# A decoder layer on one core: silu moved ahead of the quantised row on ScalarE, the output norm's scalars first on GpSimd, and one query row tile normed in every step

## The reference, cut to what matters

```
x = x + attn(layernorm(x))     # gated linear scan along the rows (stage 1)
x = x + xattn(layernorm(x))    # 16 heads over 64 context rows and one null key; output projected and normed
x = x + ffn(layernorm(x))      # gate = silu(quant(z) @ ternary(w_gate).T); up likewise;
                               # out = quant(gate * up) @ ternary(w_down).T
quant(v): scale = 127 / max|v| of the row; round(v * scale) / scale
```

## Time and profile before

| | |
|---|---|
| median of 3 runs | 540.6 us (540.0 to 541.85) |
| the profiled execution, its own time | 540.44 us |
| its span | 538.7 us |
| PE busy | 481.4 us (89% of the span) |
| DVE busy | 423.9 us (79%) |
| ACT busy | 324.0 us (60%) |
| POOL busy | 304.4 us (57%) |

### The profile page before, as it was taken

One profiled execution on the slowest core, in us unless ns is written; L12 is line 12 of the kernel. 1 busy time (PEld: TensorE's weight loads), 2 busy tenths in 40 slices (PEclk: granted clock), 3 DMA queues, 4 the chain that ended last, 5 costly groups with the idle time before them and its releaser, 6 DMA issues.

```text
span 538.7 us, 9271 instructions
## 1 busy us (share of the span) xinstructions
PE 481.4 (89%) x2926; PEld 389.4 (72%) x2954; DVE 423.9 (79%) x936; ACT 324.0 (60%) x450; POOL 304.4 (57%) x482
## 2 busy tenths in 40 slices
PE   1889999989988989999999999999999999988662
PEld 0666787767767878788887887888878778866321
DVE  4899998968337676988888888888888888875673
ACT  4422233245333353797788888877878888685451
POOL 2211223710001668778778787887787878787631
PEclk9999999999999999999999999999999999998895
DMA  8995000240000000012321222121213211212242
GB/s 263 321 337 213 1 0 1 40 78 1 2 0 1 1 2 5 12 24 50 42 49 35 44 48 49 35 50 41 49 35 46 48 46 36 54 40 63 51 97 68
DMA packets 68173, 32.06 MB, mean 60 GB/s; under 512 B 50720, under 2 KB 66336, under 8 KB 68128
## 3 DMA queue, kind: packets, MB, share of 16 engines
q1 hardware_dynamic: 68128, 31.50, 23.3%
HBM read 15.24 MB, written 4.19 MB: 36 GB/s over the span
## 4 chain that ended last, share of the span: by engine, by line
POOL 31%; issue 23%; PE 21%; DVE 17%; DMA 4%; ACT 2%; POOLq 1%; DVEq 1%; SPq 0%; ACTq 0%
PE psum L1140 9%; POOL region_d L540 5%; POOL region_d L518 3%; POOL xs L520 3%; POOL region_d L516 3%; PE psum L1156 3%; POOL sc L563 3%; POOL sc L550 3%; DVE region_a L877 3%; PE psum L1382 2%; POOL region_d L574 2%; PE psum L1387 2%; POOL region_d L531 2%; POOL region_c L579 2%; DMA region_d<-region_d 2%
## 5 line engine op out<-in xcount | busy, mean ns | idle before, releaser
L528 POOL TENSOR_TENSOR region_d<-region_d,rden 128x1024 f32<-128x1024 f32 x32 | 60.9, 1902 | 100.7 <-DVE rden L1008 100.7
L1140 PE MATMUL psum<-Mhi,xT2hi 128*128 128x260 f32 x256 | 75.0, 293 | 0.2
L1140 PE MATMUL psum<-Mlo,xT2hi 128*128 128x260 f32 x256 | 72.4, 283 | 0.0
L1140 PE MATMUL psum<-Mhi,xT2lo 128*128 128x260 f32 x256 | 72.3, 282 | 0.0
L1382 PE MATMUL psum<-VW,region_d 128*128 128x256 f32 x256 | 62.6, 389 | 4.6 <-DVE pTn L1057 4.6
L1387 PE MATMUL psum<-VW,region_d 128*128 128x256 f32 x256 | 60.7, 380 | 0.0
L1021 DVE SCALAR_TENSOR_TENSOR region_c<-psum,zw,region_c 128x1024 f32<-128x1024 f32 x29 | 37.2, 1283 | 28.7 <-ACT region_c L698 28.7
L1382 PEld LDWEIGHTS psum<-VW,region_d 128*128 128x128 f32 x256 | 49.0, 193 | 14.9 <-DVE pTn L1057 6.0
L1387 PEld LDWEIGHTS psum<-VW,region_d 128*128 128x128 f32 x256 | 49.0, 191 | 6.8
L686 ACT ACTIVATE region_d<-psum,sc 128x256 f32<-128x256 f32 x32 | 18.0, 564 | 55.7 <-POOL sc L567 54.8
L991 DVE TENSOR_REDUCE mx<-psum 128x8 f32<-128x520 f32 x64 | 44.2, 691 | 6.4 <-PE psum L1140 5.2
(11 more groups left out here) (143 smaller groups left out, 1242.2 us busy)
## 6 DMA issues: line engine op xcount, KB each, us to landing
out_dram<-xs SPq DMA_DIRECT2D x32, 128.0 KB, 1.9
xs<-in_x_dram SPq DMA_DIRECT2D x1, 2560.0 KB, 13.9
VW<-in_L_xattn_Wkv_dram SPq DMA_DIRECT2D x1, 2048.0 KB, 11.9
region_b<-in_L_xattn_Wkv_dram SPq DMA_DIRECT2D x1, 2048.0 KB, 17.6
xs<-in_x_dram SPq DMA_DIRECT2D x3, 512.0 KB, 7.0
region_w<-in_L_ffn_w_gate_dram SPq DMA_DIRECT2D x2, 512.0 KB, 10.3
region_w<-in_L_ffn_w_up_dram SPq DMA_DIRECT2D x2, 512.0 KB, 7.9
region_w<-in_L_ffn_w_down_dram SPq DMA_DIRECT2D x8, 128.0 KB, 4.5
```

The lines of the kernel that those rows point to most:

```text
L528: pool.tensor_tensor(p2[:, v, 0:H * MK].rearrange("p (h j) -> p h j", j=MK), e[:, :, 0:MK], rden[:, v, :].unsqueeze(2).broadcast_to([P, H, ...
L1140: mm = pe.matmul(dst, lhsT, rhs, start=i == 0, stop=i == len(terms) - 1)
```

## The change: what it does

1. silu and the hidden row of a tile now share one buffer, and there are two of these, taken in turn (`hid3`: the two places that were `sg` and `h`). DVE multiplies in place. silu waits for `hq_done` of the tile two before in place of `h_ready` of the one before; DVE's wait for `hq_done` ahead of the hidden row is gone, with the last tiles' detour through `e`.
2. ACT issues silu ahead of the quantised row in all steps, as it did from step 32.
3. POOL issues the output norm's three small operations (L561 to L567) ahead of the feed-forward norm's (L548 to L554).
4. ACT norms one query tile (n+5) in every step from -1 to 26, where it normed two (n+4, n+5) in each even one. The transposes stay in even steps.

```diff
-        sg3 = c["sg"]
+        hid3 = [c["sg"], c["h"]]
...
-        h3 = [c["h"], s["e"][:, 0:FI]]
...
 POOL, stages2_3:
+                if exists(n, T):
+                    ... (L558 to L568 as they were, moved up)
                 if exists(n - 2, T):
                     ... (L543 to L555)
-                if exists(n, T):
-                    ... (L558 to L568)
...
 ACT, silu_gate:
-                if positive(n - 5):
-                    act.wait_ge(h_ready, n - 5)
-                act.activation(sg3, banks(0, 2).rearrange("p b n -> p (b n)"), ACT.Silu,
+                if positive(n - 6):
+                    act.wait_ge(hq_done, n - 6)
+                act.activation(hid3[v], banks(0, 2).rearrange("p b n -> p (b n)"), ACT.Silu,
                                scale=zw[:, (n - 5) % 4, 0:1]).then_inc(silu_ready, 1)
...
 ACT, stages2_3:
-                if late(n) and exists(n - 5, T):
+                if exists(n - 5, T):
                     silu_gate(n, v)
                 if exists(n - 6, T):
...
-                    act.activation(nq3, hidden(n - 6), ACT.Copy, scale=qr[:, u, 0:1]).then_inc(hq_done, 1)
-                if not late(n) and exists(n - 5, T):
-                    silu_gate(n, v)
+                    act.wait_ge(h_ready, n - 5)
+                    act.activation(nq3, hid3[u], ACT.Copy, scale=qr[:, u, 0:1]).then_inc(hq_done, 1)
                 if not late(n) and exists(n - 3, T):
                     norm3(n, v)
-                if even:
-                    act.wait_ge(xT2_psum, half(n) + 1)
-                    norm2(n + 4, 2 * (u4 // 2))
-                    norm2(n + 5, 2 * (u4 // 2) + 1)
+                if exists(n, T - 5) or n == -1:
+                    act.wait_ge(xT2_psum, (n + 1) // 2 + 1)
+                    norm2(n + 5, (n + 5) % 4)
                 if even:
                     xT2_pair(half(n) + 2, u4 // 2)
...
 DVE, hidden_layer:
                 dve.wait_ge(silu_ready, n - 4)
-                if late(n):
-                    dve.wait_ge(hq_done, n - 6)
-                    dve.wait_ge(p_ready, 2 * T)
-                elif positive(n - 5):
-                    dve.wait_ge(hq_done, n - 5)
-                dve.scalar_tensor_tensor(out=hidden(n - 5), ..., in1=sg3, ...)
+                dve.scalar_tensor_tensor(out=hid3[v], ..., in1=hid3[v], ...)
```

More of the change, by code:

```diff
@@ L375, in late @@
             return isinstance(n, int) and n >= T
-        def hidden(n):
-            return h3[1 if isinstance(n, int) and n >= T - 5 and (n - (T - 5)) % 2 == 0 else 0]
         def half(n):
@@ L540, in stages2_3 @@
                     pool.tensor_copy(nh3, nq3).then_inc(nh_ready, 1)
+                if exists(n, T):
+                    count, = registers(pool, n + 1)
+                    pool.wait_ge(consts_set, 2)
+                    pool.wait_ge(mv3_done, count)
+                    pool.tensor_scalar(sc3[:, u, 0:1], mv3[:, u, 1:2], 1e-6, None, ALU.add).then_inc(ve3_done, 1)
+                    pool.wait_ge(ve3_done, n + 1)
+                    pool.tensor_tensor(sc3[:, u, 1:2], sc3[:, u, 0:1], expo[:, 0:1], ALU.pow).then_inc(rstd3_done, 1)
+                    count, = registers(pool, n + 1)
+                    pool.wait_ge(consts_set, 2)
+                    pool.wait_ge(rstd3_done, count)
+                    pool.tensor_scalar(sc3[:, u, 2:3], mv3[:, u, 0:1], sc3[:, u, 1:2], -1.0, ALU.mult, ALU.mult) \
+                        .then_inc(nmr3_done, 1)
                 if exists(n - 2, T):
@@ L1015, in hidden_layer @@
                 dve.wait_ge(silu_ready, n - 4)
-                if late(n):
-                    dve.wait_ge(hq_done, n - 6)
-                    dve.wait_ge(p_ready, 2 * T)
-                elif positive(n - 5):
-                    dve.wait_ge(hq_done, n - 5)
-                dve.scalar_tensor_tensor(out=hidden(n - 5), in0=banks(2, 2).rearrange("p b n -> p (b n)"),
-                                         scalar=zw[:, (n - 5) % 4, 1:2], in1=sg3, op0=ALU.mult, op1=ALU.mult) \
+                dve.scalar_tensor_tensor(out=hid3[v], in0=banks(2, 2).rearrange("p b n -> p (b n)"),
+                                         scalar=zw[:, (n - 5) % 4, 1:2], in1=hid3[v], op0=ALU.mult, op1=ALU.mult) \
                     .then_inc(h_ready, 1)
@@ L1027, in hidden_max @@
                 dve.wait_ge(h_ready, n - 4)
-                dve.tensor_reduce(amax[:, v, 0:1], hidden(n - 5), AX.X, ALU.max, apply_absolute_value=True) \
+                dve.tensor_reduce(amax[:, v, 0:1], hid3[v], AX.X, ALU.max, apply_absolute_value=True) \
                     .then_inc(hmax_done, 1)
```

## The result

The changed kernel takes 531.85 us (median of 4 runs, 531.77 to 533.52), the kernel before 540.4 beside it: a ratio of 0.985, with a 95% interval of 0.9823 to 0.9876: 1.5% faster, clear of the noise. The profiled execution took 531.91 us, its span 530.1.

A forecast was written before the change was run, and what follows sets the result against it. PE was taken as the bound, with stalls from a loop through ACT's silu, DVE and up. 540.44 less 6.4 (steps 7 to 28) and 2.4 (end) gave 531.6 profiled, 531.8 as median; own range 530 to 534, wider range 528.4 to 536.2.

The forecast's parts named there:

- The pair: An odd and an even step of the steady part together: 20.87 us in place of 21.44.
- The loop's terms: Loop from PE's projection through DVE's statistics and scores' subtraction to up: 0.11, 2.83 (even 2.85), 2.82, 4.61; sum 10.37 odd, 10.39 even.
- Rival A: The PE floor: DVE's loop shorter than counted, odd steps 10.06, pairs 20.56, time 528.4 us; chance 10%.
- Steps 7 to 28: Steady part: eleven odd steps at 10.37 and ten even at 10.50, 219.1 us in place of 225.5, 6.4 less.
- silu's 0.5 to spare: After the swap, DVE would reach the projection's statistics at 5.13, PE end the projection at about 5.57: 0.5 us margin.
- The table load: ACT's load ahead of silu: 1.28 us, the skill page's further drain of about 1.38 left out as unseen in the trace.
- Rival E: The drain after a table load makes silu 1.38 us later than counted, 0.8 more per step, 545; chance 1%.
- The query norm: One ACT query norm per step, taken at nothing; second norm done at about 5.5, PE's transposes asking at 5.7.
- Rival B: Half the gain: something else, such as query norm or silu, late by a few tenths; some 535.5 us; chance 17%.
- POOL's order: Output norm's scalars 1.36 us earlier; without it up to 0.18 per even step, about 2 in all; costs 1.06 at the end.
- The end: From step 28's end on: 1.7 from silu and output norm, 1.8 from PE's clock, less 1.06 for POOL: 2.4 us gained.

The follow-up runs named there:

- stats_late: The changed kernel with DVE's statistics of the projection behind the hidden row's maximum instead of ahead of it: 531.15 us.
- best: The changed kernel with DVE's hidden-row and quantised-input maxima ahead of the projection's statistics, ACT's query norm ahead of its feed-forward norm, POOL's old order in step 31: 526.84 us.
- norm3_first: The changed kernel with ACT's feed-forward norm ahead of silu up to step 31: 532.1 us.
- silu_undone: The kernel before with POOL's new order and the spread query norms, but the old buffers and the quantised row ahead of silu: 538.67 us.
- order_only: The kernel before with silu ahead of the quantised row, but one buffer each for silu and hidden row and the old waits: 539.66 us.
- act_old_end: The changed kernel with silu behind the quantised row in steps 30 and 31 alone: 533.19 us.
- buffers_only: The changed kernel with silu behind the quantised row up to step 31: 539.15 us.
- pool_old_end: The changed kernel with POOL's old order from step 31 on: 532.29 us.

## Why the prediction was right, and where it was not

**The pair.** 20.87 was forecast and 20.87 measured. From one L1378 to the next it is 10.40 out of an odd step and 10.48 out of an even one, in the mean of steps 12 to 22 (10.37 and 10.50 forecast). The loop's terms hold (0.10 from L1378's end to L1081, 2.82 from L984 to up), and stats_late shows by taking L1081 out of the way that this loop is what delayed up. Rival A is excluded for the change as it is, and is what best reaches.

**Steps 7 to 28.** 219.84, where 219.1 was forecast. Nearly all of the 0.8 is two steps (from L1045 to L1045): 9 to 10 took 10.83 and 23 to 24 10.85, in place of 10.49. In the second it is the gap ahead of L1087.

**silu's 0.5 to spare** holds (norm3_first). The wait in its place ahead of L1081 is 0.52 to 0.56 in most even steps (0.4 to 0.5 forecast; 0.9 behind the gaps of steps 9 and 23), but 0.20 in odd ones. There I overlooked one link: L1074, between hidden row and statistics, needs the feed-forward norm of ACT, which ends at 408.67; L1074 starts at 408.71:

```profile
408.08 0.59 ACT L701 ACTIVATE region_d<-xs,sc 128x256 f32<-128x256 f32 x1
```

The norm has kept its place, 5.0 behind L1360 (L1372) before and after, while the hidden row comes 1.1 earlier; so the norm now ends last. The overlooked link cost nothing, since L1081 waits for PE behind it.

**The table load.** I left out the drain that "ScalarE: Activation LUTs" of the Trainium skill (What ACT_TABLE_LOAD costs) adds to a switch. The trace after bears me out and not the page: the load starts 0.02 after the copy ahead of it and silu 0.01 after the load. Rival E is excluded with it. (Its 545 was also summed too low: 0.8 in each of 21 steps is 17, or 548.6.)

```profile
414.20 0.58 ACT L742 ACTIVATE region_d<-psum 128x512 f32<-128x512 f32 x1
414.80 1.28 ACT L688 ACT_TABLE_LOAD   x1
416.09 1.11 ACT L693 ACTIVATE region_c<-psum,zw 128x1024 f32<-128x1024 f32 x1
```

**The query norm, the step that failed.** "Bounds -1 and +1 us, taken at nothing": it is worth 3.2. I priced it against the order of before, where it is indeed worth nothing (silu_undone), and not against the order after the swap. The total came out because the prediction counted on the second norm being done "at about 5.5" with PE asking "at 5.7". The trace has 5.51 and 5.75, but the 5.5 holds only with one norm in a step; with two it is 6.0. The sum was right and its attribution wrong: of the 6.4 forecast for steps 7 to 28, all but POOL's 2 was booked to silu, and silu's swap alone brings 0.8. Rival B had named this margin as one that might fail.

**POOL's order.** Forecast: without it up to 0.18 in an even step, 2 us; measured 0.07 in a pair, 0.7, because the output norm's lateness mostly falls where up is late anyway. Its price at the end, 1.06 forecast, is 1.10. That it also carries 1.09 of the gain in steps 28 to 31 was in the forecast only as "the output norm no longer in the way".

**The end.** 1.43 came back in steps 28 to 31 (1.7 forecast), and 1.69 with the projection at 1.99 in place of 3.52 (1.8 forecast). The second is right in size by luck, as its reason is not supported. I let the shorter gaps keep the clock up, and leaned on "TensorE: Matmul & The Clock Gate" of the Trainium skill (Part 1), which has the clock follow how busy PE has been recently. The runs show gaps of 1.41 and 0.68 with the projection at 1.99 as well as at 3.31, and 0.34, 0.45 and 0.68 with 3.61. Some 1.5 of the 8.6 us between the two spans is thus what these executions happened to meet. By the medians, which mix such executions, the 8.5 stands: norm3_first, with the changed kernel's pace, has 532.1 over six runs.

**Left out.** Step 4 comes 0.41 earlier (208.13 for 208.54), the output norm again; the steps before 7 were taken at nothing. The rest of the end, also taken at nothing, came 0.50 shorter. These 0.92 make up for the 0.74 that steps 7 to 28 fell short of their 6.4, which was luck too. And the earlier trace rows show two long waits but not the longest of the kernel before, POOL's for `rden` (L528 for L1008, 31.1 us in 23 waits); nothing in the sum hung on it.

## What to carry to other kernels

Price each part of a change against the order that the other parts make, not against the order of before: one stall can cover another further on in the same step, and neither part shows anything until both are gone. A job whose own time does not move becomes the last to end when what it feeds comes earlier, as both norms did here. So list for each job on the engine when it ends and when its result is asked for, after the change. When a wait is gone, the next bound is a loop that can be summed from the timeline, term by term, and here it came within 0.03 us.

## What the hardware did that I had not expected

The first eight projection matmuls of step 31 took 1.99 us in ten of the thirteen profiled executions and 3.31 to 3.61 in three (before, order_only, best), and the idle time just ahead does not sort them. The mean granted clock (the number ahead of the last two columns) of order_only and of act_old_end inside the same matmuls:

```profile
492.90:494.60 1.70, 1.70 (x6) 1.38 (x7) 0.45 (x2) 1.70 (x2) 1.15 (x2) 0.61 0.41 115
```

```profile
486.20:487.90 1.70, 1.70 (x8) 1.52 (x9) 0.49 (x2) 1.70 (x3) 1.54 (x3) 1.00 0.18 39
```

1.00 is the 2.4 GHz level, 0.61 a mean that lies mostly at the 1.2 GHz one. The same happens from step 0 to 1, which takes 9.47 in ten executions and 10.57 to 11.05 in three (buffers_only, silu_undone, pool_old_end). Its first microseconds in pool_old_end, at 0.57, where the changed kernel has 1.00:

```profile
172.30:176.00 3.70, 3.70 (x16) 3.39 (x16) 1.78 (x4) 0.96 (x2) 0.00 (x0) 0.57 0.00 0
```

Both may be behind the scatter of the runs, 18 of 23 runs of the kernel before lying near 538.5, 540.2 or 542.3; that isn't shown, since only one execution of each kernel has a trace. What decides is open.

DVE loses 0.3 to 0.4 us around the statistics in two steps (9 and 23). In step 23 it is the gap of 0.47 between L1081 and L1087, which depends on it; no engine is named for it. It isn't chance: both gaps are there, in the same two steps, in all eight kernels whose DVE runs in the changed kernel's order. The three with DVE as before (before, order_only, silu_undone) have neither, and the two with DVE reordered (stats_late, best) have only one of 0.46 in step 9. So it goes with DVE's program; nothing was tried on it, and the cause is open.
